# Fetching the experts' rows in bunches behind the first steps of the last stage, not one per tile

## The chip, the cores and the metric

The kernel runs on one core of a Trainium2 chip. The metric is the device time of one execution in microseconds (us); lower is better. All times of the trace are microseconds from the start of the profiled span.

## What is computed

Two gated layers over 64 sequences of 64 tokens with 128 features, 4096 tokens in all. The change touches the seam between the first layer's mixture of experts and the second layer.

```
def _L0_ffn_ref(...):
    top_id = jnp.argmax(x @ gate_w, axis=-1)
    ...
    routed = jnp.einsum('eth,te->th', y, onehot)      # one of 8 experts per token
    shared = _swiglu(x, sh_gate, sh_up, sh_down)
    return (shared + routed)

x = x + tanh(g_xattn[0]) * _L0_xattn_ref(_layernorm(x), ctx, ...)
x = x + tanh(g_ffn[0])   * _L0_ffn_ref(_layernorm(x), ...)
x = x + tanh(g_xattn[1]) * _L1_xattn_ref(_layernorm(x), ctx, mask, ...)   # pooled context + x @ W_in
x = x + tanh(g_ffn[1])   * _L1_ffn_ref(_layernorm(x), ...)                # top 2 of 8 experts
```

## The kernel before

The tokens are 32 tiles of 128 (NT = 32), one token to a partition. The kernel has three stages: attention with routing (scattering the tokens, sorted by expert, into a buffer in DRAM), the experts over the sorted tiles (their rows are stored to `sorted_y`), and the last stage, which is the second layer; some work of the stages overlaps. Each engine runs its own program in program order, and semaphores order the engines among each other.

The last stage is a software pipeline written by hand. Every engine walks through 44 steps; in step s it does its part for tile s - k, where k is the lag that `stage(k)` names. The parts that matter here, with their lines:

- GpSimd (POOL), `last_step`: it fetches the expert's rows of a tile with an indirect DMA (L641, `gather`), adds them to X (L659, tile s), and then does the small arithmetic of two layer norms in one go (L672 `vv`, L674 `nm`, L677 `roots`, L681 `shifts`): for tile s - 2 the norm in front of the pooled attention, for tile s - 6 the norm in front of the last experts. From step 4 on it adds the pooled context (L687, tile s - 4). At step 2 it also computes 16 columns of an inverse root (L619, `crms_power`). Before the steps it waits until all expert tiles are stored, and fetches tiles 0, 1 and 2.
- VectorE (DVE), step s: statistics of X for tile s - 1 (L1279, L1288, after the add L659), then the residual add L1283 and the statistics L1292 and L1301 for tile s - 6, the choice of two experts for tile s - 9 (L1296 to L1328, the last one writes `mask1`), the masked copies `z` for tile s - 10 (L1310, tile vp), the output add L1321 for tile s - 12. It waits for the `shifts` of POOL's step s - 1 ahead of L1288, and POOL's `vv` of step s waits for L1301 of DVE's step s.
- ScalarE (ACT): the two normalized copies (L869, L874) after `shifts`, and copies out of PSUM.
- TensorE (PE): eight spreads of the mask for tile s - 10 (L1702), small matmuls and transposes (L1711 to L1720), sixteen matmuls of 128 x 128 for tile s - 11 (L1725), the bias (L1730, L1734) and the routing of tile s - 9 (L1694). The step whose L1702 is for tile m is step m + 10.

In the first nine steps PE, ACT and DVE have other work as well, written ahead of or between their parts (`filling`): the shared expert of the first layer for the second half of the tokens, and the pooling of the context. POOL has no part of that. The order of that work, the lags and the fetch distance (`AHEAD = 3`: step s fetches tile s + 3 before it adds tile s) are all fixed in the code. Each fetch counts up one of four semaphores `y_in`, tile t on number t % 4, and the add of tile s waits for its own.

Of the kernel before, what the change touches and what calls it, by code (L numbers as in the profile page):

```python
# [71 lines left out]
def walk(eng, tiles, depth, step, before_loop=None, unroll=TURN, lead=None, early=None, drain=None,  # L72
         looped=True):

    first = -(-depth // unroll) * unroll
    assert tiles % unroll == 0 and tiles > first

    def peeled(s):
        step(lambda lag: Tile(s - lag) if 0 <= s - lag < tiles else None)

    for s in range(first):
        if lead:
            lead(s)
        peeled(s)
        if early:
            early(s)
    if before_loop:
        before_loop()
    if looped:
        with eng.Fori(0, (tiles - first) // unroll) as turn:  # L90
            for k in range(unroll):
                step(lambda lag: Tile(first + k - lag, turn, unroll))
    else:
        for s in range(first, tiles):
            peeled(s)
    for s in range(tiles, tiles + depth):
        peeled(s)
        if drain:
            drain(s - tiles)


def walk_flat(tiles, depth, step):

    for s in range(tiles + depth):
        step(lambda lag: Tile(s - lag) if 0 <= s - lag < tiles else None)


def flamingo_gated_two_layers(nc, x, ctx_k, ctx_v_swapped, consts, gates, w_qkv, w_proj, b_proj, gate_w,
                              sh_gate_up, sh_down, rt_gate_up, rt_down, patch_mask, w_in, b_in, g_res, g_init,
                              router_w, router_b, expert_w, expert_b, out):  # L110
    NT = x.shape[1] // P
# [12 lines left out]
    LAGS = 6  # L124
    REGION = NT * P + P
    SPARE = NS - NT
    AHEAD = 3

    with ExitStack() as ctx:
        def sb(name, shape, dt=F32):  # L130
# [2 lines left out]
        def sem(name):  # L133
            return ctx.enter_context(nc.semaphore(name))
# [246 lines left out]
        y_in = [sem(f"y_in{c}") for c in range(4)]  # L381
# [16 lines left out]
        def arrived(eng, sems, tile):  # L398

            if tile is not None and tile.turn is None:  # L400
                for c, (lo, _) in enumerate(TILE_CHUNKS):
                    if tile.n == lo:
                        eng.wait_ge(sems[c], 16 if c < 2 else 48)
                        eng.nop(nofuse=True)
# [82 lines left out]
        def _(pool):  # L487
# [128 lines left out]
            def crms_power(part):  # L616
                columns = part.stop - part.start
                pool.wait_ge(crms_step, 2)
                pool.tensor_tensor(crms[:, part], crms[:, part], halfneg[:].to_broadcast([P, columns]), ALU.pow)\  # L619
                    .then_inc(crms_step, 1)  # L620
# [16 lines left out]

            walk(pool, NS, 6, load_weights_and_store, drain=context_scales)

            def gather(t):  # L640
                pool.indirect_dma_start(out=XN2[:, t, 0:D], out_offset=None, in_=sorted_y,  # L641
                                        in_offset=bass.IndirectOffsetOnAxis(ap=places[:, t:t + 1], axis=0))\
                    .then_inc(y_in[t % 4], 16)

            pool.wait_ge(places_known, 1)
            for done in stored:
                pool.wait_ge(done, 16 * (NS // 4))
            for t in range(AHEAD):
                gather(t)

            def last_step(stage):
                x, v, f, a = (stage(i) for i in (0, 2, 4, 6))
                if x:
                    if x.t + AHEAD < NT:
                        gather(x.t + AHEAD)
                    if x.slot == 0:
                        pool.wait_ge(S["h_added"], Tile(x.quad).done())
                    pool.wait_ge(y_in[x.slot], 16 * (x.quad + 1))
                    pool.tensor_tensor(X[:, x.cols(D)], X[:, x.cols(D)], XN2[:, x.t, 0:D], ALU.add)\  # L659
                        .then_inc(S["l_x2"], 1)  # L660
                if v or a:

                    turn = v.done() if v else a.done() + 4
                    both = slice(0 if v else 1, 2 if a else 1)
                    par = (v or a).par
                    if v:
                        pool.wait_ge(S["l_moments"], v.done())
                        pool.wait_ge(S["l_hn_ready"], v.freed())
                    if a:
                        pool.wait_ge(S["l_moments2"], a.done())  # L670
                        pool.wait_ge(S["l_normed"], a.freed())
                    pool.tensor_tensor(vv[:, par, both], mm[:, par, both, 1], two_eps[:, both], ALU.add)\  # L672
                        .then_inc(S["l_vars"], 1)
                    pool.tensor_tensor(nm[:, par, both], mm[:, par, both, 0], minus[:, both], ALU.mult)\  # L674
                        .then_inc(S["l_means"], 1)
                    pool.wait_ge(S["l_vars"], turn)
                    pool.tensor_tensor(roots[:, par, both], vv[:, par, both], halves[:, both], ALU.pow)\  # L677
                        .then_inc(S["l_roots"], 1)
                    pool.wait_ge(S["l_means"], turn)
                    pool.wait_ge(S["l_roots"], turn)  # L680
                    pool.tensor_tensor(shifts[:, par, both], nm[:, par, both], roots[:, par, both], ALU.mult)\  # L681
                        .then_inc(S["l_shifts"], 1)
                if f:
                    pool.wait_ge(S["l_hn_ready"], f.done())
                    if f.slot == 0:
                        pool.wait_ge(S["c_put"], Tile(f.quad).done())
                    pool.tensor_tensor(X[:, f.cols(D)], X[:, f.cols(D)], DP[:, f.cols(D)], ALU.add)\  # L687
                        .then_inc(S["l_added"], 1)
                if x and x.t == 2:
                    crms_power(slice(4 * CT, NT))  # L690

            walk_flat(NT, 12, last_step)


# [1110 lines left out]
```

## Time and profile before

| | |
|---|---|
| timed runs, median (lowest to highest) | 494.19 us (491.52 to 498.88), 3 runs |
| profiled execution, span from first to last instruction | 490.0 us; the profile gives no other time of its own for it |
| PE, DVE, POOL, ACT busy over the span | 443.7, 366.8, 319.4, 277.8 us |
| mean granted TensorE clock over the span | 0.972 of full speed |
| last stage | POOL's first fetch at 333.57 us, its last at 446.04 us; the last DVE output add begins at 487.75 us |

Busy time is an average over stages with different limits, so what a change in the last stage is worth is read from rows inside it. In the timeline a row gives start, duration, engine, line, operation, tiles and, in brackets, the idle time of the engine just before it and what ended it.

### The profile page before, as it was taken

The page shows a single profiled execution, that of the slowest core. Times are in us where ns is not written, and L with a number is a line of the kernel's source. Part 1 is how long each engine was busy: PE and PEld are TensorE (multiplying, and loading weights), DVE is VectorE, ACT ScalarE, POOL GpSimd, SP SyncE. Part 2 cuts the span into 40 slices and gives each one's busy share as a digit, 9 for nine tenths or more (in the row PEclk, how much of TensorE's full clock was granted, in tenths as well). Part 3 has the DMA queues.
Part 4 walks back from the last instruction along what each step waited for, and adds up shares of the span by engine and source line. Part 5 has one row for each costly group of instructions (what it writes and reads, how often), then busy time and mean ns, then how long its engine had stood idle before and what let it go on. Part 6 is the DMA issues. An engine that isn't in the chain of part 4 may idle for free. (4 is left out here: it accounts for less than half of the span.)

```text
span 490.0 us, 20510 instructions
## 1 busy us (share of the span) xinstructions
PE 443.7 (91%) x6871; PEld 349.2 (71%) x6872; DVE 366.8 (75%) x1201; ACT 277.8 (57%) x775; POOL 319.4 (65%) x780
## 2 busy tenths in 40 slices
PE   5789999989999999997987999987997799899998
PEld 3456677756766666774666988864655799898997
DVE  3668999978898989944768666545766678788984
ACT  2468899877988888764234545434233434444431
POOL 3845765567777777767723666577825899898630
PEclk9889999998999999989999999998999699999999
DMA  7941231111111110100245776631000011111001
GB/s 232 413 152 41 48 36 27 26 31 40 28 32 33 30 36 22 37 20 18 76 131 158 228 227 216 222 121 37 18 5 13 16 46 33 46 37 37 23 23 33
DMA packets 37394, 37.38 MB, mean 76 GB/s; under 512 B 20440, under 2 KB 31504, under 8 KB 36816
## 3 DMA queue, kind: packets, MB, share of 16 engines
q0 software_dynamic: 7552, 20.20, 12.9%
q1 hardware_dynamic: 29200, 16.06, 11.9%
q8 instruction: 39, 0.64, 0.6%
q10 hardware_dynamic: 576, 0.26, 0.2%
q14 instruction: 27, 0.22, 0.1%
HBM read 24.82 MB, written 7.86 MB: 67 GB/s over the span
## 5 line engine op out<-in xcount | busy, mean ns | idle before, releaser
L979 DVE TENSOR_REDUCE negm<-PS 128x4 f16<-128x512 f32 x128 | 81.9, 681 | 0.4
L716 ACT ACTIVATE pexp<-PS 128x512 f32<-128x512 f32 x128 | 69.4, 595 | 6.4 <-PE PS L1383 5.8
L1725 PE MATMUL PS<-w,vp 128*128 128x128 f32 x512 | 63.3, 277 | 0.0
L1725 PEld LDWEIGHTS PS<-w,vp 128*128 128x128 f32 x512 | 60.6, 194 | 0.0
L1396 PEld LDWEIGHTS PS<-pexp,vp 128*32 128x32 f32 x2048 | 34.5, 113 | 26.4 <-issue 20.5
L1396 PE MATMUL PS<-pexp,vp 128*32 128x64 f32 x2048 | 50.3, 230 | 0.3
L1619 PE MATMUL PS<-xsT,wst 128*128 128x128 f32 x320 | 44.4, 282 | 3.0 <-DVE stack L1217 1.3
L1619 PEld LDWEIGHTS PS<-xsT,wst 128*128 128x128 f32 x320 | 38.8, 191 | 7.3 <-issue 5.0
L581 POOL DMA_INDIRECT sorted_x<-VALL,posu x32 | 33.3, 1040 | 13.4 <-issue 7.6
L611 POOL DMA_DIRECT2D wst<-in_rt_gate_up_dram x40 | 21.5, 538 | 29.2 <-PE PS L1619 19.9
L1310 DVE TENSOR_TENSOR vp<-PS,xnT 128x1024 f32<-128x1024 f32 x32 | 38.6, 1205 | 0.8 <-PE PS L1702 0.8
L641 POOL DMA_INDIRECT VALL<-sorted_y,places x32 | 32.5, 1015 | 7.2 <-issue 7.2
L1217 DVE TENSOR_TENSOR stack<-PS,oS 128x256 f32<-128x256 f32 x40 | 16.9, 423 | 22.8 <-ACT oS L828 22.7
L828 ACT ACTIVATE oS<-PS 128x256 f32<-128x256 f32 x40 | 15.4, 385 | 31.7 <-PE PS L1619 31.1
L888 ACT CAST mask1T<-PS 96x128 bf16<-96x128 f16 x32 | 8.4, 262 | 41.9 <-PE PS L1734 41.6
L1566 PE MATMUL PS<-wqkv,xnT 128*128 128x384 f32 x64 | 31.3, 573 | 0.4 <-ACT xnT L739 0.4
L522 POOL TENSOR_TENSOR ve<-mv,epsc 128x1 f32<-128x1 f32 x32 | 6.1, 190 | 37.8 <-DVE mv L1015 37.6
L1367 PE MATMUL PS<-ktp,qc 32*64 32x128 f16 x1024 | 26.9, 221 | 3.8 <-DVE negm L979 1.7
L1633 PE MATMUL PS<-rdn,stack 128*128 x160 | 25.6, 282 | 4.6 <-DVE stack L1217 3.5
L869 ACT ACTIVATE on<-X,shifts,roots 128x128 f32<-128x128 f32 x32 | 15.7, 492 | 22.5 <-POOL shifts L681 21.2
L614 POOL DMA_DIRECT2D sorted_y<-YS x40 | 21.8, 546 | 9.4 <-DVE YS L1213 4.7
L1383 PE MATMUL PS<-qc,ktp 32*128 32x64 f16 x1024 | 25.9, 189 | 1.6 <-DMA qc<-mT 1.6
(246 smaller groups left out, 1254.5 us busy)
## 6 DMA issues: line engine op xcount, KB each, us to landing
wst<-in_rt_gate_up_dram POOLq DMA_DIRECT2D x40, 256.0 KB, 3.5
xs<-sorted_x SPq DMA_DIRECT2D x40, 64.0 KB, 2.8
sorted_y<-YS POOLq DMA_DIRECT2D x40, 64.0 KB, 3.0
out_dram<-X SPq DMA_DIRECT2D x32, 64.0 KB
X<-in_x_dram SPq DMA_DIRECT2D x1, 1536.0 KB, 8.2
CK<-in_ctx_k_dram SPq DMA_DIRECT2D x1, 1536.0 KB, 12.2
CV<-in_ctx_v_swapped_dram SPq DMA_DIRECT2D x1, 1536.0 KB, 16.6
rdn<-in_rt_down_dram POOLq DMA_DIRECT2D x1, 1024.0 KB, 10.6
```

The source lines that it names most:

```text
L581: pool.indirect_dma_start(out=sorted_x, out_offset=bass.IndirectOffsetOnAxis(ap=posu[:, o.t:o.t + 1], axis=0), in_=XN2[:, o.t, :], in_offs ...
L641: pool.indirect_dma_start(out=XN2[:, t, 0:D], out_offset=None, in_=sorted_y, in_offset=bass.IndirectOffsetOnAxis(ap=places[:, t:t + 1], ax ...
L716: nc.scalar.activation(pexp[:, j, :], PS[:, 2 + j % 2, :], ACT.Exp).then_inc(S["exped"], 1)
L979: dve.tensor_reduce(negm[:, a.par, :, j], PS[:, j % 2, :].rearrange("p (g k) -> p g k", g=G), AX.X, ALU.max, negate=True).then_inc(S["maxe ...
L1310: dve.tensor_tensor(z[:, m.par], PS[:, 4:6, :].rearrange("p b (e t) -> p (b e) t", t=P), xnT4[:, m.slot, :].unsqueeze(1).to_broadcast([P, ...
L1367: last = nc.tensor.matmul(PS[64 * b:64 * b + 64, hg % 2, g * P:g * P + P], qc[rows, a.slot, g, 64 * b:64 * b + 64], kt[rows, a.slot, b, g, :],
L1383: last = nc.tensor.matmul(PS[:, 2 + hg % 2, at:at + SEQ], kt[rows, b.slot, seq, g, :], qc[rows, b.slot, g, SEQ * seq:SEQ * seq + SEQ], sta ...
L1396: last = nc.tensor.matmul(PS[32 * g:32 * g + 32, 7, j * P + SEQ * seq:j * P + SEQ * seq + SEQ], vp[:, b.par, seq, g * HG + j, :], pexp[:, ...
L1566: nc.tensor.matmul(PS[:, 4, P:4 * P], xnT[:, f.par, :], wqkv[:], start=True, stop=True)\
L1619: last = nc.tensor.matmul(PS[:, 2 + s.par, i * P:i * P + P], wst[:, s.slot, i * P:i * P + P], xsT[:, s.par, :], start=True, stop=True)
L1633: last = nc.tensor.matmul(PS[:, 6 + b.par, 0:D], act2T[:, b.par, i * P:i * P + P], rdn[:, ds(e_down * FF + i * D, D)], start=(i == 0), sto ...
L1725: nc.tensor.matmul(PS[:, 6 + y.par, 0:D], z[:, y.par, e, :], w1[:, e * D:e * D + D], start=(e == 0), stop=False)
```

## The change

The fetches of tiles 0 to 3 stay where they were. Then the fetch of later tiles goes from the head of each step (one, for the tile three steps ahead) to the end of the first nine steps, in bunches: behind step 0 tile 4, behind step 1 tile 5, behind step 2 tiles 6 to 8, behind step 3 tiles 9 to 11, behind step 4 tiles 12 to 15, behind step 5 tiles 16 to 21, behind step 6 tiles 22 to 26, behind step 7 tiles 27 to 30, behind step 8 tile 31. From step 9 on POOL fetches nothing. The tiles share semaphores in six groups (`Y_GROUPS`), and the add waits once per group, at its first tile, for all of the group's fetches: at tiles 0, 1, 3, 7, 13 and 21. The number of fetches and the rows that they bring are the same.

```
-    AHEAD = 3
+    FETCHED = [4, 5, 6, 9, 12, 16, 22, 27, 31] + [NT] * NT
+    Y_GROUPS = [(0, 1), (1, 3), (3, 7), (7, 13), (13, 21), (21, NT)]
...
+            def fetched_with(t):
+
+                g = [lo <= t < hi for lo, hi in Y_GROUPS].index(True)
+                return y_in[g % 4], 16 * sum(hi - lo for lo, hi in Y_GROUPS[g % 4:g + 1:4])
+
             def gather(t):
                 pool.indirect_dma_start(out=XN2[:, t, 0:D], out_offset=None, in_=sorted_y,
                                         in_offset=bass.IndirectOffsetOnAxis(ap=places[:, t:t + 1], axis=0))\
-                    .then_inc(y_in[t % 4], 16)
+                    .then_inc(fetched_with(t)[0], 16)
...
-            for t in range(AHEAD):
+            for t in range(3):
                 gather(t)
...
                 if x:
-                    if x.t + AHEAD < NT:
-                        gather(x.t + AHEAD)
+                    if x.t == 0:
+                        gather(3)
                     if x.slot == 0:
                         pool.wait_ge(S["h_added"], Tile(x.quad).done())
-                    pool.wait_ge(y_in[x.slot], 16 * (x.quad + 1))
+                    if any(x.t == lo for lo, _ in Y_GROUPS):
+                        pool.wait_ge(*fetched_with(x.t))
                     pool.tensor_tensor(X[:, x.cols(D)], X[:, x.cols(D)], XN2[:, x.t, 0:D], ALU.add)\
                         .then_inc(S["l_x2"], 1)
...
                 if x and x.t == 2:
                     crms_power(slice(4 * CT, NT))
+                if x:
+                    for t in range(FETCHED[x.t], FETCHED[x.t + 1]):
+                        gather(t)
```

## Rows read from the trace of the kernel before

**Rows 1.** The page's chain that ended last, by engine and by line.

```profile
POOL 9%; PE 8%; issue 4%; DVE 1%; POOLq 0%; ACT 0%; DVEq 0%; ACTq 0%
PE PS L1725 5%; POOL roots L677 3%; POOL X L659 2%; PE PS L1702 1%; POOL X L687 1%; POOL VALL L641 1%; POOL shifts L681 1%; POOL vv L672 1%; POOL nm L674 1%; DVE vp L1310 0%; PE PS L1715 0%; PE PS L1694 0%; PE PS L1720 0%; ACT on L869 0%; DVE str_ L1292 0%
```

**Rows 2.** Windows of the last stage: length, engines' busy time (x instructions), clock, DMA.

```profile
336.00:382.00 46.00, 40.95 (x242) 26.23 (x242) 30.22 (x75) 15.55 (x45) 28.02 (x55) 0.95 0.07 17
382.00:391.00 9.00, 7.57 (x56) 7.04 (x57) 6.11 (x26) 3.00 (x11) 8.02 (x21) 0.58 0.08 22
...
403.00:452.00 49.00, 44.72 (x474) 43.79 (x474) 39.47 (x174) 21.23 (x73) 43.81 (x102) 1.00 0.15 39
452.00:488.00 36.00, 35.72 (x384) 35.40 (x381) 29.30 (x108) 11.82 (x41) 11.96 (x40) 1.00 0.10 27
```

**Rows 3.** PE's timeline, L1702 of steps 10, 12, 16, 30 and 36.

```profile
382.04 1.01 PE L1702 MATMUL PS<-ident,mask 128*128 128x128 f16 x8
...
390.76 0.61 PE L1702 MATMUL PS<-ident,mask 128*128 128x128 f16 x8
...
403.32 0.61 PE L1702 MATMUL PS<-ident,mask 128*128 128x128 f16 x8 [0.17 <-DVE mask L1328]
...
451.54 0.61 PE L1702 MATMUL PS<-ident,mask 128*128 128x128 f16 x8 [0.28 <-DVE mask L1328]
...
469.81 0.61 PE L1702 MATMUL PS<-ident,mask 128*128 128x128 f16 x8
```

**Rows 4.** POOL's timeline at its last fetch: steps 28 and 29.

```profile
446.04 1.03 POOL L641 DMA_INDIRECT VALL<-sorted_y,places  x1 [0.16 <-issue]
447.09 0.46 POOL L659 TENSOR_TENSOR X<-X,VALL 128x128 f32<-128x128 f32 x1
...
449.26 0.46 POOL L659 TENSOR_TENSOR X<-X,VALL 128x128 f32<-128x128 f32 x1
```

**Rows 5.** POOL's waits from 336 to 382 us: total, times, longest.

```profile
POOL vv L672 <- DVE mm L1301: 13.0, 3, 9.1
...
POOL vv L672 <- DVE mm L1288: 1.4, 1, 1.4
```

**Rows 6.** POOL's timeline: two fetches in a row and the add of step 0.

```profile
336.23 0.94 POOL L641 DMA_INDIRECT VALL<-sorted_y,places  x1 [0.30 <-issue]
337.48 0.94 POOL L641 DMA_INDIRECT VALL<-sorted_y,places  x1 [0.30 <-issue]
338.43 0.47 POOL L659 TENSOR_TENSOR X<-X,VALL 128x128 f32<-128x128 f32 x1
```

**Rows 7.** POOL's timeline, first and last of eight scatters in a row.

```profile
234.84 0.99 POOL L581 DMA_INDIRECT sorted_x<-VALL,posu  x1 [0.72 <-DVE VALL L974]
...
244.26 0.97 POOL L581 DMA_INDIRECT sorted_x<-VALL,posu  x1 [0.30 <-DVE texp L1115]
```

**Rows 8.** POOL's timeline of steps 2, 3, 4 and 9, without the fetches.

```profile
343.22 2.91 POOL L619 TENSOR_TENSOR crms<-crms,halfneg 128x16 f32<-128x16 f32 x1
...
347.40 0.47 POOL L659 TENSOR_TENSOR X<-X,VALL 128x128 f32<-128x128 f32 x1
...
348.82 0.19 POOL L681 TENSOR_TENSOR shifts<-nm,roots 128x1 f32<-128x1 f32 x1
...
350.55 0.47 POOL L659 TENSOR_TENSOR X<-X,VALL 128x128 f32<-128x128 f32 x1
...
352.11 0.45 POOL L687 TENSOR_TENSOR X<-X,CV 128x128 f32<-128x128 f32 x1
...
381.76 0.46 POOL L659 TENSOR_TENSOR X<-X,VALL 128x128 f32<-128x128 f32 x1
...
383.48 0.45 POOL L687 TENSOR_TENSOR X<-X,CV 128x128 f32<-128x128 f32 x1
```

**Rows 9.** DVE's timeline: the end of its step 6.

```profile
367.65 0.18 DVE L1301 BATCH_NORM_AGGREGATE mm<-str_ 128x2 f32<-128x6 f32 x1
```

**Rows 10.** All fetches (L641), time from issue to landing.

```profile
DMA to landing us min/median/max: 2.4/2.6/4.3
```

## The prediction

> **What bounds the kernel now.** I read the chain that ended last first, because only work on it can move the end. It lies on POOL and PE, in lines that are all of the last stage [rows 1]. Then I cut that stage into windows [rows 2] and laid PE's steps against POOL's.
>
> From 403 to 452 us POOL is busy 43.81 of 49 us, PE 44.72, DVE 39.47 [rows 2]. Busy time alone doesn't say which of them sets the pace. PE's steps do: from step 16 (403.32) to step 30 (451.54) a step takes 48.22 / 14 = 3.44 us, and at both ends PE waits for DVE's mask; from step 30 to step 36 (469.81), when POOL has no fetch left, 18.27 / 6 = 3.045 us, with no wait [rows 3]. POOL shows why. A step with a fetch has 0.16 us of idle and 1.05 us up to the add, together 1.21 us, for the fetch, and from the add of step 28 to that of step 29, which has no fetch, it takes 2.17 us [rows 4]. 1.21 + 2.17 is 3.4 us, the pace of the stretch. So there POOL is the limit, and without the fetch it would be PE at 3.045 us: DVE's 39.47 us are 2.8 us a step.
>
> From 336 to 382 us, the steps 0 to 8, it is the other way round. PE is busy 40.95 of 46 us with the shared expert and the context, POOL only 28.02 [rows 2], and POOL waits 13.0 + 1.4 = 14.4 us for DVE [rows 5]. The change moves POOL's fetches from the stretch that POOL limits into this one. The question is whether 14.4 us are room enough.
>
> **What is taken away.** From step 9 on no fetch is left. PE went from step 12 (390.76) to step 30 in 60.8 us; at PE's own pace those 18 steps take 18 x 3.045 = 54.8 us, a gain of 6.0 us. This is the most that there is to win. Steps 12 to 16 took 12.56 us, 3.14 each, already nearly PE's pace [rows 3], so not all the stage was limited by POOL. The waits on `y_in` fall from 32 to 6; the adds followed their fetch without idle [rows 4, 6], so I count them at nothing.
>
> **What is put in.** Up to the add of step 9, POOL issued the fetches of tiles 0 to 12; after the change it issues all 32 up to there, 19 more. What does one cost inside a bunch? Two fetches in a row begin 1.25 us apart, 0.94 of work and 0.30 of idle, and the next add begins only when the fetch has ended [rows 6]: POOL can't do anything else meanwhile. Eight scatters in a row, the same kind of DMA in the other direction, are (244.26 - 234.84) / 7 = 1.35 us apart [rows 7]. I take 1.30 and keep 1.25 and 1.35 as ends.
>
> Here a rule of the Trainium skill speaks for the change. "DMA: Bandwidth & Descriptors", section "Anatomy of one DMA — SWDGE (gpsimd) path", says that on GpSimd's path the fixed cost is mostly the wait for completion, and that many descriptors can be emitted before their cost shows. By it the followers in a bunch would be nearly free. The rows above say otherwise: each one holds POOL for over a microsecond. What the Trainium skill's rule would give is the second rival below.
>
> **POOL's time line after the change.** Up to step 2 nothing moves: the fetches of tiles 4 and 5 come ahead of the adds of steps 1 and 2 as before. The L619 of step 2 ends at 343.22 + 2.91 = 346.13 us [rows 8]. From there to the add of step 9 POOL has to do
> - the work of steps 3 to 8 without fetches: step 3 is 347.40 to 349.01, 1.61 us; steps 4 and 5 as 350.55 to 352.56, 2.01 us each; steps 6 to 8, with both norms, as step 9 from 381.76 to 383.93, 2.17 us each [rows 8]. Sum 1.61 + 4.02 + 6.51 = 12.1 us;
> - 26 fetches (tiles 6 to 31) in seven bunches: 7 that follow arithmetic at 1.21 [rows 4] and 19 followers at 1.30, 8.5 + 24.7 = 33.2 us.
>
> If it never waits, the add of step 9 begins at 346.1 + 12.1 + 33.2 = 391.5 us, against 381.76: 9.7 us later (8.8 and 10.7 us with 1.25 and 1.35). The check from the other side: 19 more fetches are 24.7 us, less the 14.4 us of waits that they fill, 10.3 us.
>
> Does it never wait? The long wait was for L1301 of DVE's step 6, which ends at 367.83 [rows 9]. By the same sum POOL's add of step 6 comes at 346.1 + 1.6 + 4.0 + 4 x 1.21 + 12 x 1.30 = 372.2 us, so DVE is done long before. From there DVE's steps wait for POOL, not the other way: its step s needs the add of step s - 1 and the `shifts` of step s - 1. Nor for landing: the one tight group is that of tiles 3 to 6, whose last fetch is issued at 346.3 and lands by 348.9 (350.6 at worst) [rows 10], where the add of step 3 comes at 349.9; at most 0.7 us, and I take none. All later groups are waited for two steps or more behind their last fetch.
>
> Who is behind that? In program order DVE has the statistics of tile s - 1 ahead of everything else of a step, so its step 9 starts with the add of POOL's step 8, and with it the first mask and PE's first L1702, which came 0.3 us after the add of step 9 [rows 3, 8]. ACT's part of the shared expert stands behind its copies of the norms as well; that moves PE's last `filling` by some 2 us, which end long before 391 and cost nothing.
>
> **The sum.** PE's step 12 came 9.0 us after POOL's add of step 9 [rows 3, 8]. Nothing in those steps gets shorter, since DVE still waits for POOL's `shifts`, and PE's clock is low there: the granted clock averages 0.58 from 382 to 391 us [rows 2], the two levels being 1.2 and 2.4 GHz; L1702 takes 1.01 us at step 10 and 0.61 at step 12 [rows 3]. So step 12 comes at about 400.5, step 30 at 455.3 instead of 451.5 us, and from there all is as before. -6.0 + 9.7 = +3.7 us: a span of 493.7 us. The three timed runs have their median 4.2 us above the profiled span; I carry that and predict 497.9 us, 0.8% slower. About 2% is what a measurement of this kernel can tell from no change, so this counts as the same.
>
> The bounds: the fetch inside a bunch gives -0.9 to +1.0 us. PE's pace was 3.045 without waits and 3.14 from step 12 to 16; 0.1 x 18 gives up to +1.7 us. The clock: PE has little to do from about 383 to 391 us after the change, so it is low again when step 10 comes. If it recovers a step sooner or later than before, a step of 4.4 us (8.72 / 2 from step 10 to 12) [rows 3] becomes one of 3.05 or the reverse: 1.3 us either way. Together the span changes by +1.5 to +7.7 us, times from 495.7 to 501.9 us.
>
> **The rivals.**
> - *The pace doesn't improve.* POOL, DVE and PE wait for each other in a ring (`shifts` to L1288 and L1301, to `vv`, to `shifts`), and the ring might hold 3.44 us a step without the fetch too. Then only the delay is left: 490.0 + 9.7 = 499.7 us, a time of 503.9, the limit of 2%. For it speaks that every member shows idle time in that stretch; against it that POOL's step 28 to 29 took 2.17 us [rows 4] and PE ran at 3.045 after it.
> - *The bunch is cheap.* If followers cost POOL nothing, 7 bunches are 7 x 1.21 us, as much as the 7 fetches that steps 3 to 9 had, the add of step 9 stays at 381.76, and the gain of 6.0 us is whole: 484.0 us, a time of 488.2, 1.2% faster. The spacings of fetches and scatters in a row speak against it [rows 6, 7]. Between this and the forecast lie all cases in which a follower takes less than 1.30 us: the delay falls to 6.0 us, and the change breaks even, at 1.30 - 3.7 / 19 = 1.1 us.
> - *The bunch is dear*, the side beyond 2%. Fetches that pile up could hold each other up, as the landing of 4.3 us against a median of 2.6 hints [rows 10]. Each 0.1 us on a follower costs 1.9 us; from 1.62 us on, 0.32 more than I take, the change loses 9.8 us and ends above 504 us. It would need a quarter more than any mean spacing that the trace shows.
>
> **How the numbers follow.** The forecast gets 0.70, the pace that doesn't improve 0.08, the dear bunch 0.08, the cheap one or one near it 0.14. The range reaches from 491 us (the forecast's lower end, and somewhat over half of the way from there to the cheap bunch) to 503 us. Nothing but a cheap bunch and a quick clock together would pass 2% on the fast side: 0.02. Slower by over 2%: half of each of the two slow rivals, and a little for an addition of the forecast's upper bounds, 0.10. The rest, 0.88, is within 2%.
>
> **What would show it.** Right: POOL without waits from 346 us to the add of step 9 near 391.5; fetches 1.25 to 1.35 us apart; PE's first L1702 near 391.8 and step 12 near 400.5; 3.05 us a step from there, POOL at some 2.2 us of work a step with waits for DVE. Wrong: a first L1702 before 388 us (the bunch is cheaper), a pace above 3.2 us from step 12 on (the ring), L1702 at 1.01 us beyond step 12 (the clock), or adds that idle for landing.

## The result and the profile after

The change makes the kernel slower by 1.0%: the ratio of the new time to the old is 1.0101, with a 95% interval of 1.007 to 1.0132 (medians 496.62 and 491.29 us, 20 runs each). A second set of runs, beside other kernels on another occasion, gave 1.008 (1.0047 to 1.0112). Of 491.3 us these are +5.0 us (3.4 to 6.5) and +3.9 us (2.3 to 5.5). +3.7 us was forecast. This is less than the 2% by which the prediction tells two times apart, so it counts as the same there, but both intervals lie above 1.

Some executions of either kernel are slower by some 2%: the medians are of all runs, the ratio leaves these out, and since the first profile of the changed kernel is of one, slowed ahead of the last stage, the lines below are from the profile taken with the second set; its span is 491.0 us. POOL's fetch is now L647, its add L666, the spreads on PE are L1712.

POOL's timeline, its first fetch, the end of step 6 and steps 7 to 10:

```profile
331.39 1.08 POOL L647 DMA_INDIRECT VALL<-sorted_y,places  x1 [1.31 <-issue]
...
374.74 0.94 POOL L647 DMA_INDIRECT VALL<-sorted_y,places  x1 [0.30 <-issue]
375.99 0.94 POOL L647 DMA_INDIRECT VALL<-sorted_y,places  x1 [0.31 <-issue]
377.23 0.94 POOL L647 DMA_INDIRECT VALL<-sorted_y,places  x1 [0.30 <-issue]
378.19 0.47 POOL L666 TENSOR_TENSOR X<-X,VALL 128x128 f32<-128x128 f32 x1
...
379.92 0.45 POOL L694 TENSOR_TENSOR X<-X,CV 128x128 f32<-128x128 f32 x1
380.54 1.03 POOL L647 DMA_INDIRECT VALL<-sorted_y,places  x1 [0.16 <-issue]
...
387.68 1.02 POOL L647 DMA_INDIRECT VALL<-sorted_y,places  x1 [0.17 <-issue]
388.73 0.47 POOL L666 TENSOR_TENSOR X<-X,VALL 128x128 f32<-128x128 f32 x1
...
390.86 0.45 POOL L666 TENSOR_TENSOR X<-X,VALL 128x128 f32<-128x128 f32 x1
```

Inside a bunch a fetch begins every 1.25 us, as the two in a row did before [rows 6], and each bunch stands ahead of the next add. The add of step 9 (388.73) comes 57.3 us behind POOL's first fetch (331.39); before, that was 381.76 - 333.57 = 48.2 us [rows 8]. From there on there is no fetch, and the next add comes 2.13 us later.

POOL's waits from 344.0 to 388.5 us (total, times, longest), and DVE's from 369 to 389:

```profile
POOL VALL L647 <- issue: 7.3, 26, 0.5
```

```profile
DVE st L1289 <- POOL X L666: 6.7, 3, 5.1
DVE X L1080 <- PE PS L1447: 3.1, 1, 3.1
DVE mm L1298 <- POOL shifts L688: 2.6, 3, 0.9
...
```

This is [rows 5] turned round. POOL waits for nobody any more; the 7.3 us are the gaps ahead of its 26 fetches. DVE waits for POOL's adds instead.

PE's timeline, L1712 of steps 10, 11, 12, 29 and 30, and windows of the stage:

```profile
389.00 1.01 PE L1712 MATMUL PS<-ident,mask 128*128 128x128 f16 x8
393.14 1.01 PE L1712 MATMUL PS<-ident,mask 128*128 128x128 f16 x8 [0.64 <-DVE mask L1338]
398.31 0.61 PE L1712 MATMUL PS<-ident,mask 128*128 128x128 f16 x8
...
449.68 0.61 PE L1712 MATMUL PS<-ident,mask 128*128 128x128 f16 x8
452.69 0.61 PE L1712 MATMUL PS<-ident,mask 128*128 128x128 f16 x8
```

```profile
344.00:388.70 44.70, 31.35 (x172) 20.54 (x171) 22.82 (x60) 12.98 (x38) 36.46 (x61) 0.87 0.13 38
389.00:398.00 9.00, 7.56 (x47) 7.03 (x47) 6.43 (x26) 2.86 (x9) 6.24 (x19) 0.52 0.03 7
398.00:453.00 55.00, 54.99 (x607) 54.93 (x605) 52.73 (x217) 26.28 (x92) 36.73 (x108) 1.00 0.08 24
453.00:488.00 35.00, 35.00 (x382) 34.95 (x380) 28.96 (x107) 12.11 (x42) 11.83 (x39) 1.00 0.09 25
```

From step 12 to step 30 PE takes 54.4 us, 3.02 a step, and is busy 54.99 of 55 us, where before it needed 60.8 us [rows 3] and was busy 44.72 of 49 [rows 2]. POOL's busy time there falls to 36.73 of 55 us. So the change does both things that it can do: the later stretch gets shorter by 6.4 us, and it begins later by more than that.

### The profile page after: what moved, and what is told of

Same layout as the page of the kernel before. It is cut to its first block, busy times and chain, and to the rows that moved or that the text cites. A ratio compares the mean times of both kernels' runs of the same rounds, so it can differ in the third digit from the quotient of the medians.

```text
span 501.9 us, 20503 instructions
## 1 busy us (share of the span) xinstructions
PE 451.4 (90%) x6871; PEld 354.1 (71%) x6872; DVE 371.0 (74%) x1201; ACT 277.9 (55%) x775; POOL 317.0 (63%) x780
## 4 chain that ended last, share of the span: by engine, by line
PE 44%; POOL 21%; issue 15%; DVE 10%; DMA 4%; ACT 2%; POOLq 2%; DVEq 1%; ACTq 1%
PE PS L1735 12%; POOL VALL L647 6%; PE PS L1406 4%; PE PS L1576 3%; PE PS L1712 3%; PE PS L1629 3%; POOL rstd L554 2%; PE PS L1594 2%; PE PS L1377 2%; PE PS L1393 2%; POOL vp L544 2%; PE PS L1476 2%; DMA qc<-mT 2%; POOL vp L542 2%; DMA sorted_x<-VALL,posu 2%
## 5 line engine op out<-in xcount | busy, mean ns | idle before, releaser
L1406 PEld LDWEIGHTS PS<-pexp,vp 128*32 128x32 f32 x2048 | 35.3, 115 | 29.3 <-issue 21.5
L1406 PE MATMUL PS<-pexp,vp 128*32 128x64 f32 x2048 | 51.7, 234 | 1.2 <-DVE isel L962 0.5
L647 POOL DMA_INDIRECT VALL<-sorted_y,places x32 | 31.0, 969 | 9.8 <-issue 9.8
L1576 PE MATMUL PS<-wqkv,xnT 128*128 128x384 f32 x64 | 32.9, 599 | 0.4 <-ACT xnT L749 0.4
L1377 PE MATMUL PS<-ktp,qc 32*64 32x128 f16 x1024 | 28.0, 229 | 3.7 <-DVE negm L989 2.1
```

The costliest lines, as they stand in the source:

```text
L1377: last = nc.tensor.matmul(PS[64 * b:64 * b + 64, hg % 2, g * P:g * P + P], qc[rows, a.slot, g, 64 * b:64 * b + 64], kt[rows, a.slot, b, g, :],
L1406: last = nc.tensor.matmul(PS[32 * g:32 * g + 32, 7, j * P + SEQ * seq:j * P + SEQ * seq + SEQ], vp[:, b.par, seq, g * HG + j, :], pexp[:, ...
L1576: nc.tensor.matmul(PS[:, 4, P:4 * P], xnT[:, f.par, :], wqkv[:], start=True, stop=True)\
```

## The experiments

My theory: a fetch costs POOL 1.25 us wherever it stands; in the first nine steps POOL has some 14.4 us of waits that can hold fetches for nothing, and what goes beyond is lost; behind step 12 POOL's fetch sets the pace, until it falls below PE's 3.0 us. The rivals: a ring of waits that holds the pace anyway; a bunch that costs nothing, or more than its fetches; the place of the bunches and not their number.

The table shows where the kernels stood: "extra" is the number of fetches beyond the old 13 up to the add of step 9, then the ratio to the kernel before with its 95% interval, and, from the profiles, the time in us from POOL's first fetch to the add of step 9, to PE's step 12 and step 30, and to the end of the span.

| kernel | extra | ratio | add of step 9 | step 12 | step 30 | end |
|---|---|---|---|---|---|---|
| before | 0 | 1 | 48.2 | 57.2 | 118.0 | 156.4 |
| `no_late_fetch` | 0 | 0.9871 (0.9823 to 0.9919) | 48.0 | 57.4 | 111.8 | 150.1 |
| `extra_fetches` | 19 | 1.0213 (1.0154 to 1.0271) | 57.5 | 67.3 | 128.9 | 167.2 |
| `changed_again` | 19 | 1.008 (1.0047 to 1.0112) | 57.3 | 66.9 | 121.3 | 159.6 |
| `one_bunch` | 19 | 1.0128 (1.0077 to 1.0179) | 59.9 | 69.1 | 123.6 | 162.0 |
| `fourteen_extra` | 14 | 0.9979 (0.9931 to 1.0026) | 51.5 | 60.9 | 115.2 | 153.5 |
| `fit_into_waits` | 9 | 0.9879 (0.9799 to 0.9959) | 48.1 | 57.4 | 111.9 | 150.2 |
| `same_number_earlier` | 9 | 0.9899 (0.9865 to 0.9934) | 47.4 | 57.5 | 112.1 | 150.3 |
| `four_extra` | 4 | 0.9949 (0.9908 to 0.9989) | 49.7 | 59.3 | 116.6 | 155.3 |

**The gain by itself.**

```
-                    if x.t + AHEAD < NT:
+                    if x.t + AHEAD < 13:
                         gather(x.t + AHEAD)
...
-                    pool.wait_ge(y_in[x.slot], 16 * (x.quad + 1))
+                    if x.t < 13:
+                        pool.wait_ge(y_in[x.slot], 16 * (x.quad + 1))
```

> The kernel before, with the fetches of tiles 13 to 31 left out (their rows are not added; the adds read what lies in the tile), and with the waits for them. It measures the gain alone: the first nine steps are as before, from step 10 on POOL fetches nothing. My theory, that POOL's fetch sets the pace from step 12 to 30: PE at 3.0 us a step there, 6 us less (5 to 7), ratio near 0.988. The rival, that a ring of waits holds 3.44 us a step without the fetch too: no change.

Measured 0.9871, 6.3 us less. Step 12 comes where it did, and the 18 steps to step 30 take 54.4 instead of 60.8 us. There is no ring that holds 3.44 us a step: taking POOL's fetch away is enough to put PE at its own pace.

**The delay by itself.**

```
+    EXTRA = [0, 0, 0, 2, 4, 7, 12, 16, 19]
...
+            def extra(k):
+                to = wst[:, k // 4, k % 4 * D:k % 4 * D + D] if k < 16 else xs[:, k - 16, :]
+                pool.indirect_dma_start(out=to, out_offset=None, in_=sorted_y,
+                                        in_offset=bass.IndirectOffsetOnAxis(ap=places[:, 13 + k:14 + k], axis=0))\
+                    .then_inc(wst_in[0], 16)
...
+                if x and 1 <= x.t <= 7:
+                    for k in range(EXTRA[x.t], EXTRA[x.t + 1]):
+                        extra(k)
...
+            pool.wait_ge(wst_in[0], 16 * (NS // 4 + 19))
```

> The kernel before, and 19 more fetches of 128 rows into tiles that nobody reads any more, behind steps 2 to 7 in bunches of 2, 2, 3, 5, 4 and 3; the 32 fetches stay one per step. It measures the delay alone. My theory, that each follower holds POOL for 1.25 us and 14.4 us of waits swallow a part: add of step 9 some 9.5 us later, 9 us more in all (8 to 11), ratio near 1.019. The rival, that a bunch costs POOL next to nothing: 0 to 2 us.

Measured 1.0213, 10.5 us more. The bunch behind step 6 in its timeline:

```profile
372.76 1.02 POOL L654 DMA_INDIRECT wst<-sorted_y,places  x1 [0.16 <-issue]
374.09 0.95 POOL L654 DMA_INDIRECT wst<-sorted_y,places  x1 [0.30 <-issue]
375.34 0.95 POOL L654 DMA_INDIRECT wst<-sorted_y,places  x1 [0.30 <-issue]
376.59 0.95 POOL L654 DMA_INDIRECT wst<-sorted_y,places  x1 [0.30 <-issue]
```

Four more fetches hold POOL 5 us, though nobody reads what they bring. The add of step 9 is 9.3 us late, as in the changed kernel; by step 30 it is 10.9, since this kernel has POOL's slow pace behind it and recovers nothing. Delay and gain together, +10.5 and -6.3, make +4.2 us: the change is the sum of its two halves.

**The changed kernel beside it.** Nothing is edited.

> The changed kernel itself, beside the kernel before on the same chip, for an undisturbed profile of it. By what was measured: ratio 1.007 to 1.013; add of step 9 some 57.3 us behind POOL's first fetch, PE at 3.0 us a step from step 12 on.

1.008, and 57.3 us: as expected; its lines stand above.

**As many fetches as the waits hold.** Each kernel of this and the next three groups has its own list, and groups that follow its bunches; four semaphores were too few for these, so they also use those of two earlier transfers.

```
-    FETCHED = [4, 5, 6, 9, 12, 16, 22, 27, 31] + [NT] * NT
+    FETCHED = [4, 5, 6, 7, 8, 9, 16, 19, 21, 22, 22, 23, 23, 24, 24, 25, 25, 26, 26, 27, 27, 28, 28, 29, 29, 30, 30, 31, 31, 32] + [NT] * NT
...
-                return y_in[g % 4], 16 * sum(hi - lo for lo, hi in Y_GROUPS[g % 4:g + 1:4])
+                k = g % 12
+                return (y_in + stored + wst_in)[k], 16 * sum(hi - lo for lo, hi in Y_GROUPS[k:g + 1:12]) + (k >= 4) * 16 * (NS // 4)
```

> The changed kernel with another list: one fetch per step up to step 4, then 7, 3, 2 and 1 behind steps 5 to 8, which is 9 more than before up to the add of step 9 and about what POOL's waits there can hold; the other ten one behind every second step from step 10 to step 28. Groups follow the bunches. My theory: the add of step 9 stays within 1 us of before, POOL has 2.2 + 0.6 = 2.8 us a step behind that, less than PE's 3.0, so the gain of 6 us stays: ratio 0.987 to 0.990. If the waits of the first nine steps were not free room, 9 x 1.25 = 11 us would be lost: ratio near 1.01.

Measured 0.9879 (0.9799 to 0.9959): faster than both kernels, and not told apart from the one that fetches nothing late. Its window from 389 to 443 us, and the same one of `no_late_fetch`:

```profile
389.00:443.00 54.00, 54.00 (x588) 53.90 (x586) 52.05 (x213) 25.52 (x89) 45.08 (x116) 1.00 0.12 34
```

```profile
389.00:443.00 54.00, 53.99 (x591) 53.93 (x590) 52.26 (x214) 25.56 (x91) 36.67 (x108) 1.00 0.08 24
```

POOL is busy 45.08 of 54 us with every second step's fetch in it, and PE still runs without a gap. A late fetch costs nothing as long as POOL's load stays below PE's.

**The same number in another place.** The list is set against that of `fit_into_waits`.

```
-    FETCHED = [4, 5, 6, 7, 8, 9, 16, 19, 21, 22, 22, ...]
+    FETCHED = [4, 5, 6, 10, 14, 18, 19, 20, 21, 22, 22, ...]
```

> As fit_into_waits, 9 extra fetches up to the add of step 9, but behind steps 2, 3 and 4 (4 each), where POOL had no wait, and one behind each of steps 5 to 8. My theory, that only the number counts as long as POOL has caught up by step 6, where it waited 9 us: the same as fit_into_waits within 2 us. The rival, that place counts because ACT and DVE stand behind POOL's norms of the steps 3 to 5 with their other work: several us more than fit_into_waits.

Measured 0.9899, 1 us beside `fit_into_waits` and well inside its interval. The extra fetches stand where POOL had no wait, so it reaches step 6 later, and its long wait there, 9.1 us before, is gone; of all its waits for DVE, 2.3 us are left, at steps 7 and 8. With so few fetches, place makes no difference that can be seen.

**Numbers between.**

```
-    FETCHED = [4, 5, 6, 9, 12, 16, 22, 27, 31] + [NT] * NT
+    FETCHED = [4, 5, 6, 8, 10, 12, 18, 22, 25, 27, 27, 27, 28, 28, 28, 29, 29, 29, 30, 30, 30, 31, 31, 31, 32] + [NT] * NT
```

> The changed kernel with 14 instead of 19 extra fetches up to the add of step 9 (2, 2, 2, 6, 4, 3 and 2 behind steps 2 to 8), the last five behind every third step from step 11 on. My theory, that the waits hold 14.4 us and each extra fetch of 1.25 us beyond that is lost: 14 x 1.25 - 14.4 = 3 us of delay less 6 us of gain, so 3 us faster than before, ratio 0.994, between the list with nine (0.988) and the change (1.010). A rival, that bunches of five or six are what hurts, not their number: near the change, 1.005 or more.

Measured 0.9979 (0.9931 to 1.0026), so 1.0 us faster where 3 us were expected, and not told apart from either the forecast or no change; it isn't the 1.005 of the rival. The profile is clearer: the add of step 9 is 3.3 us late, as worked out, with POOL's last waits just gone (0.4 us from 340 to 388), and the end comes 2.9 us earlier than before. Fourteen fetches cost 3.3 us and nineteen 9.1: 5.8 us for five, 1.16 each. Nine cost nothing.

```
-    FETCHED = [4, 5, 6, 9, 12, 16, 22, 27, 31] + [NT] * NT
+    FETCHED = [4, 5, 6, 7, 8, 9, 12, 14, 16, 17, 18, 19, 19, 20, 21, 22, 23, 23, 24, 25, 26, 27, 27, 28, 29, 30, 31, 31, 32] + [NT] * NT
```

> The same with 4 extra fetches up to the add of step 9 (3, 2, 2 and 1 fetches behind steps 5 to 8) and the other 15 behind four of every five steps from step 9 on. My theory: no delay, and POOL needs 2.17 + 0.79 x 1.21 = 3.1 us a step behind step 9, still its limit but only just above PE's 3.0: 60.8 - 18 x 3.13 = 4.5 us faster, ratio 0.991. If what counted were the bunching and not POOL's load per step, the gain would stay near 4/19 of 6 us: 0.997.

Measured 0.9949 (0.9908 to 0.9989), 2.5 us less; the expected 0.991 is at the edge of the interval, and 0.997 lies inside it too, so the time doesn't decide. The profile has 57.3 us from step 12 to 30, 3.18 a step. That is 3.5 of the 6.4 us, not 4 / 19 of them, with PE waiting a little again:

```profile
391.00:448.00 57.00, 55.29 (x592) 54.89 (x590) 50.25 (x216) 26.13 (x89) 50.28 (x121) 1.00 0.13 37
```

The 3.18 us are a little more than the expected mean load of 3.13, which is uneven: 3.4 us in four steps and 2.2 in the fifth. POOL waited 1.8 us for ACT and DVE in that window; whether the unevenness is the cause was not tried. The add of step 9 is 1.5 us late, where no delay was expected. Four fetches don't explain that, since POOL still waited 10.8 us for DVE ahead of it; the last section shows what moved.

**All in one bunch.**

```
-    FETCHED = [4, 5, 6, 9, 12, 16, 22, 27, 31] + [NT] * NT
+    FETCHED = [4, 5, 6, 7, 8, 9, 29, 30, 31, 32] + [NT] * NT
```

> The same 19 extra fetches as the change, but in one bunch: 20 fetches behind step 5, one each behind steps 6, 7 and 8. My theory, that the number counts and POOL has no wait in either: as the change or up to 3 us slower, because DVE's and ACT's share of steps 7 and 8 now comes behind the bunch in one go: ratio 1.010 to 1.016. If the split over several steps was what delayed DVE and ACT, it would be faster than the change.

Measured 1.0128, 2.4 us above `changed_again` by the two ratios, with intervals that overlap. ACT's and DVE's longest waits from 355 to 396 us:

```profile
ACT on L880 <- POOL shifts L689: 17.4, 3, 14.2
...
```

```profile
DVE st L1290 <- POOL X L667: 10.3, 2, 9.9
DVE pexp L1075 <- ACT stack L800: 7.3, 4, 2.7
DVE X L1081 <- PE PS L1448: 3.1, 1, 3.1
```

ACT stands 14.2 us behind a norm of POOL, and its last part of the shared expert behind that. PE's last down product needs that part, and DVE waits 3.1 us for the product ahead of its share of step 8. So POOL does get a wait back in this kernel, 2.5 us for DVE at step 8; that is the 2.5 us by which the add of step 9 is later than in the changed kernel. Beyond the free room, splitting the bunch helps by that much in the profiles, and the timed runs don't tell it from nothing; it doesn't decide the sign.

## Why the prediction was right

The measured 496.62 us lie beside the forecast 497.9, and its sign holds. That the time itself came so near is in part luck. The forecast stood on three runs of the kernel before, with a median of 494.19 us; over 20 runs it is 491.29. Of the 4.2 us that were carried from span to time, 2.7 are the spread of those three runs, since the profiled one took 491.52 us with a span of 490.0, 1.5 us less. That put the forecast too high, and the change came out 1.3 us dearer than forecast by its ratio, which took part of it back. What can be held against the mechanism is the difference. Step by step:

- *POOL limits steps 12 to 30, and PE at 3.045 us would follow.* Right, by the changed kernel and by `no_late_fetch`. The gain term, 6.0 us, measured 6.4, since PE's pace without any fetch is 3.02.
- *A fetch in a bunch costs 1.30 us.* It measured 1.25, the lower end. The 19 followers of the sum are 1 us less. (By its own terms the sum is 391.4 and not 391.5 us; and 1.62 us, the price from which the bunch would be dear, is a fifth and not a quarter above the scatters' 1.35 us.)
- *POOL never waits and the add of step 9 comes at 391.5 us.* Right: behind the first fetch this is 57.9 us, and 57.3 were measured. The delay of 9.7 us came out as 9.1.
- *Nothing in steps 9 to 12 gets shorter or longer.* Nearly: 9.0 us became 9.6. The granted clock was 0.52 against 0.58 [rows 2] from step 10 to 12, the lower of the two levels for nearly all of that time, after PE had been busy for only 2.39 of the 9 us from 380 to 389, waiting behind DVE for most of the rest. It is within the 1.3 us that the bounds had for it.
- *Nothing else moves.* Right: from step 30 to the end 38.3 us, before 490.0 - 451.54 = 38.5 [rows 3].

The sum with measured terms is 9.15 + 0.58 - 6.40 - 0.15 = +3.18 us in the two profiles, with 3.9 and 5.0 us in the timed sets, whose intervals both hold the forecast 3.7.

The rivals fell one by one: the pace does improve, followers do cost POOL their full 1.25 us, and no fetch in a pile held POOL longer than one in a pair, nor did any land later (2.4 to 3.5 us in the changed kernel, 2.4 to 4.3 before [rows 10]). The rule of the Trainium skill's "DMA: Bandwidth & Descriptors", section "Anatomy of one DMA — SWDGE (gpsimd) path", that many descriptors can be emitted before their cost shows, doesn't hold here if it is read as one on POOL's own time: POOL was held 1.25 us by each fetch in the bunches of `extra_fetches`, and it waited for the landing of none of them before its last step was done.

The break-even price of a follower, 1.1 us in the prediction, is 1.0 to 1.1 with what was measured: 1.25 less 3.18 / 19 by the profiles, or less 5.0 / 19 by the first set. The prediction has no word on the number at which fetches begin to cost. By its terms 14.4 us of free room hold eleven to twelve extra fetches of 1.25 us; nine were free, and fourteen cost 3.3 us.

## What to carry to other kernels

Prefetching from an engine that issues its own DMAs moves work of that engine, not only transfers: count the issuing time of each DMA against the waits that it is meant to fill, and stop where the waits end. The rest needn't go early at all: spread it so that the engine's load per step stays just under that of the engine that sets the pace. Here nine early and ten spread fetches kept the whole gain (0.988), nineteen early ones turned it into a loss of 1%.

## What was not expected of the hardware

Where the other engines' work of the first steps stands against POOL's first fetch differs between profiles with the same code up to there. The third of the shared expert's down products on PE (L1437, in the changed kernel L1447) begins 30.4 us behind the first fetch in the profile of before and 28.9 in that of the changed kernel:

```profile
363.99 2.05 PE L1437 MATMUL PS<-shd,pexp 128*128 128x128 f32 x16
```

```profile
360.31 2.05 PE L1447 MATMUL PS<-shd,pexp 128*128 128x128 f32 x16
```

```profile
334.00:340.00 6.00, 5.61 (x22) 3.12 (x22) 3.18 (x6) 0.10 (x1) 4.91 (x6) 0.72 0.17 44
```

```profile
334.00:340.00 6.00, 5.88 (x36) 3.67 (x35) 4.38 (x10) 1.76 (x5) 5.28 (x8) 1.00 0.15 44
```

The two windows, before and changed, show the granted clock: 0.72 and 1.00 in those 6 us. Counted from the first fetch, the second window stands 2.2 us later than the first; the same stretch in the changed kernel, 331.82 to 337.82 us, shows 1.00 as well. The experiments lie between 28.9 and 31.8 us, most at 30.2, and in all ten profiles the clock of this stretch goes with it: 28.9 to 29.3 us in the three with 1.00, 30.2 to 30.5 in the six with 0.72, and 31.8 in `four_extra`, with 0.52. That the clock is the cause was not tried. Where POOL has waits left, such a shift moves the add of step 9: in the five kernels with none, four or nine extra fetches it comes 17.8 to 18.1 us behind that product. In `four_extra` the product itself is 1.3 us later than before, which is most of its 1.5 us. Where POOL has none, as in the changed kernel, the add of step 9 stays at 57.3 us in both of its profiles. A difference of one pair of profiles is not good for better than 1.5 us here.
